# Four moves in the order of work of a two-layer transformer kernel: GpSimd's products, the output projection's sum, the expert mixes, and the third query/key product

## The chip, the cores and the metric

The kernel runs on one core of a Trainium2 chip. The metric is the device time of one execution in microseconds (us). The core's engines are TensorE (PE in the profile; PEld is its weight load), VectorE (DVE), ScalarE (ACT), GpSimd (POOL) and SyncE (SP), which issues the DMAs. They run side by side, each through its own list of instructions in order, and meet at semaphores only.

## The reference

The input is 16 sequences ("rows") of 256 tokens by 128 features. Two layers follow, each an attention and a mixture of experts, with a residual sum and a layer norm behind each of the four parts. All of it is float32.

```python
x = L0_attn_x                                          # (16, 256, 128)
x = _layernorm(x + _L0_attn_ref(...))                  # RMS norm, 16 heads of 64, softmax, output projection, bias
x = _layernorm(x + _L0_ffn_ref(...))                   # a shared expert and 8 routed ones, top 2, hidden 256, gelu
x = _layernorm(x + _L1_attn_ref(...))                  # per token of (b, n, h, d): 16 heads of 8
x = _layernorm(x + _L1_ffn_ref(...))                   # 8 routed experts, top 2, hidden 512, gelu
```

```python
def _layernorm(x, axis=-1, eps=1e-05):
    m = jnp.mean(x, axis=axis, keepdims=True)
    v = jnp.var(x, axis=axis, keepdims=True)
    return (x - m) / jnp.sqrt(v + eps)
```

The second attention mixes the 16 heads of each token with one another (its scores are 16x16 for a token), so it needs no product over tokens and lies on DVE and POOL.

## The kernel before

**Pipeline over rows.** The rows go through a software pipeline of 18 iterations. Iteration `it` does, for three rows at once, part a (first attention and the up products of the first experts) of row `it`, part b (down products of the first experts, second attention, up products of the second experts) of row `it-1`, and part c (down products of the second experts) of row `it-2`. Iterations 2 to 14 are one hardware loop of 13 passes; 0, 1, 15, 16 and 17 are written out, with the parts that exist there (part a ends with iteration 15).

**Steps.** Within an iteration come eight steps `s` (0 to 7), one for each pair of heads of the first attention: scores `S{2s+2}`, `S{2s+3}` of the next pair (PE), their negated maxima `head_max` (DVE), `softmax_exp` (ACT), transposes `T` of the probabilities (PE), their copy (ACT), the product `O{s}` with the values (PE), its copy to `oT` (ACT, `o_out`), its scaling by the inverse sums (DVE, `o_scale`, L662), and the query/key product `QK{s+3}` (PE) with its split in two parts (ACT `qk_out`, DVE `lower_qk`). Between these PE does "fill" units of parts b and c: `D0p0` to `D0p3` and `D1e0` to `D1e7` are the down products of experts, which DVE weighs by the gates and adds up (`mix`, L723). `fill_out(v, s, place)` (L817) says which mixes belong to which place of a step.

**Behind the steps.** `OUT` is the output projection: 16 products of 128x128, of 8 head pairs for each of 2 blocks of tokens, summed in one PSUM bank (L1018 to L1026). DVE adds the residual `x_plus` (input plus bias, made on POOL in `plus`, L445) and takes the layer norm's statistics (`ln_stats`); POOL turns the variance into its inverse root (`inverse_std`, L424); DVE applies both (`ln_apply`, L693, its instruction is L696); PE transposes the result (`X1T`), DVE splits it in two parts (L809, L814), and the up products `U0_0` to `U0_8` follow. In between lie `D1e6`, `D1e7`, the value products `V0` to `V3` of the next row, the second attention's `AOT` and `PROJ`, its norm's transpose `X3T`, then `QK0`, `QK1` and the up products `U1_0` to `U1_15`.

**What sets the order.** PE's order is the list that `pe_units` (L62) writes; the orders of the other engines are written out in their bodies: POOL's at L477, DVE's at L828. Each PSUM bank has two semaphores, `filled` and `drained`: a unit waits until the bank's last user is drained. Banks are given in rings: `A0`, `A1` for `QK`, `O`, `HT`, `OUT`, `V`, `X1T`; `F0`, `F1` for the fill units (with `T0`, `T1` behind the steps). So `D0p3` uses the bank of `D0p2` and waits until the mix of `D0p2` has read it, and `O6` uses the bank of `O5` and waits for `o_scale(5)`.

**POOL's part of the second attention.** `value_product(v, t, halves)` (L468) multiplies the weights of one block `t` of tokens by the values, one instruction of 128x1024 for each half of the heads; those of block 1 are L471 with no sum behind them, and DVE sums them in `head_mix(v, 1, ·)`, behind the mix of `D1e7`.

Of the kernel before, what the change touches and what calls it, by code (L numbers as in the profile page):

```python
# [36 lines left out]
NT = S // P  # L37
# [24 lines left out]
def pe_units(it):  # L62

    a, b, c, nxt = it < ROWS, 1 <= it <= ROWS, 2 <= it <= ROWS + 1, it < ROWS - 1
    order = []
    rings = {"A": ["A0", "A1"], "F": ["F0", "F1"], "G": ["F0", "F1", "T0", "T1"]}
    turn = {"A": 0, "F": 0, "G": 1}

    def put(ring, *names, on=True):
        for name in names if on else ():  # L70
            banks = rings.get(ring, [ring])
            order.append((name, banks[turn.get(ring, 0) % len(banks)]))
            if ring in turn:
                turn[ring] += 1

    put("F", "D0p0", "D0p1", on=b)
    for s in range(HP):
        put("S0", f"S{2 * s + 2}", on=a and s + 1 < HP)
        put("S1", f"S{2 * s + 3}", on=a and s + 1 < HP)
        put("A", "QK2", on=a and s == 0)  # L80
        put("A", f"O{s - 1}", on=a and s >= 1)
        put("F", *fill_units(it, s, 0))
        put("T0", f"T{2 * s}", on=a)
        put("T1", f"T{2 * s + 1}", on=a)
        put("A", f"QK{s + 3}", on=a and s + 3 < HP)
        put("A", "HT", on=nxt and s == HP - 2)
        put("F", *fill_units(it, s, 1))
    put("A", f"O{HP - 1}", "OUT", on=a)
    put("F", "D1e6", "D1e7", on=c)
    put("A", "V0", on=nxt)  # L90
    put("A", "X1T", on=a)
    put("G", "V1", on=nxt)
    put("A", "V2", on=nxt)
    put("G", "U0_0", "U0_1", on=a)
    put("A", "R0", on=a)
    put("G", "U0_2", "U0_3", on=a)
    put("G", "AOT", on=b)
    put("G", "U0_4", on=a)
    put("G", "PROJ", on=b)
    put("G", "U0_5", "U0_6", "U0_7", "U0_8", on=a)  # L100
    put("A", "V3", on=nxt)
    put("G", "X3T", on=b)
    put("A", "QK0", "QK1", on=nxt)
    put("G", "U1_0", "U1_1", "U1_2", "R1", "U1_3", "U1_4", on=b)
    put("G", "U1_5", "U1_6", on=b)
    put("S0", "S0", on=nxt)
    put("S1", "S1", on=nxt)
    put("G", *[f"U1_{u}" for u in range(7, 2 * E)], on=b)
    return order
# [71 lines left out]
def transformer_blocks(nc, x_in, norm_scale, wq_in, wk_in, wv_in, wo_in, b_out_in,  # L181
# [3 lines left out]
    with ctx:  # L185
# [221 lines left out]
        @block.gpsimd  # L407
        def _(pool):
            g = nc.gpsimd
            g.memset(ident[:], 0.0).then_inc(consts_ready, 1)  # L410
            pool.wait_ge(consts_ready, 1)
            g.affine_select(out=ident[:], in_=ident[:], compare_op=ALU.not_equal, fill=1.0, base=0,
                            pattern=[[-1, P]], channel_multiplier=1)
            g.memset(minus_half[:], -0.5)
            g.memset(table_load[:], 0.0)
            for i in range(2):
                g.memset(top2[i][:], -3.0e38)
                g.memset(gates[i][:, :, E:E + 1], 1.0)
            g.memset(ln_eps[:], LN_EPS)
            g.memset(rms_eps[:], RMS_EPS)  # L420
            g.memset(one_over_d[:], 1.0 / D).then_inc(consts_ready, 1)
            pool.wait_ge(consts_ready, 2)

            def inverse_std(v, i, lag):  # L424
                pool.wait_ge(stats_ready[i], v.at(lag, 1, 1))
                settled(pool, g.tensor_tensor(var_eps[i][:], mv[i][:, :, 1], ln_eps[:], ALU.add))  # L426
                g.tensor_tensor(std_inv[i][:], var_eps[i][:], minus_half[:], ALU.pow).then_inc(std_ready[i], 1)  # L427

            def split_up_weights(group, *weights):

                pool.wait_ge(loaded[group], n_loads[group])
                for whole, (w_hi, _) in weights:
                    g.tensor_copy(w_hi[:], whole)
                pool.drain()
                for whole, (w_hi, w_lo) in weights:
                    ins = g.tensor_tensor(w_lo[:], whole, w_hi[:].bitcast(F32), ALU.subtract)  # L436
                ins.then_inc(up_split, 1)

            def rms(v):
                pool.wait_ge(sq_ready, v.at(-1, 1, 1))  # L440
                settled(pool, g.tensor_tensor(mean_sq[:], sum_sq[:], one_over_d[:], ALU.mult))  # L441
                settled(pool, g.tensor_tensor(mean_sq[:], mean_sq[:], rms_eps[:], ALU.add))
                g.tensor_tensor(rms_inv[:], mean_sq[:], minus_half[:], ALU.pow).then_inc(rms_ready, 1)  # L443

            def plus(v):  # L445
                wait_weights(pool, v, 1)
                pool.wait_ge(x_loaded, v.at(-1, 16, 16))
                if v.a:
                    pool.wait_ge(*v.drain("OUT"))
                g.tensor_tensor(x_plus[:], x_row[:], b_out[:, 0:1, :].broadcast_to([P, NT, D]), ALU.add).then_inc(xplus_ready, 1)  # L450

            def head_product(v):


                for t, i in ((0, 1), (1, 0), (1, 1))[0 if v.a else 1:]:
                    if (t, i) != (1, 1):
                        pool.wait_ge(*v.drain(f"LQ{t}"))
                    q, k = head_pairs(t, half(i))
                    settled(pool, g.tensor_tensor(prod[:, t, half(i)], q, k, ALU.mult))  # L459
                    ins = add_pairs(prod[:, t, half(i)], DH1)  # L460
                    if i == 1:
                        ins.then_inc(prod_ready, 1)

            def add_pairs(x, n):

                return g.tensor_tensor(x[:, :, :, 0:n // 2], x[:, :, :, 0:n // 2], x[:, :, :, n // 2:n], ALU.add)  # L466

            def value_product(v, t, halves=(0, 1)):  # L468
                pool.wait_ge(exp1_ready, v.at(1, NT, t + 1))
                for i in halves:  # L470
                    ins = g.tensor_tensor(pv1[:, t, half(i)], *weights_and_values(t, i), ALU.mult)  # L471
                    if t == 0:
                        pool.drain()  # L473
                    ins = add_pairs(pv1[:, t, half(i)], NH1) if t == 0 else ins
                    ins.then_inc(pv1_ready, 1)

            def body(v):  # L477
                if v.it == 0:
                    split_up_weights(2, (router0_in_sb[:], router0), (up0_loaded, up0))
                if v.next:  # L480
                    rms(v)
                if v.it == 0:
                    split_up_weights(4, (up1_loaded, up1))
                if v.b:
                    wait_weights(pool, v, 3)
                    inverse_std(v, 1, 1)
                    pool.wait_ge(ln_ready[1], v.at(1, 1, 1))
                    g.tensor_tensor(x3[:], x2[:], bproj[:, 0:1, :].broadcast_to([P, NT, D]), ALU.add).then_inc(x2plus_ready, 1)  # L488
                    head_product(v)
                    if v.a:  # L490
                        value_product(v, 0)
                    value_product(v, 1, (0,))
                if v.a:
                    inverse_std(v, 0, 0)
                if v.b:
                    value_product(v, 1, (1,))
                if v.c:
                    inverse_std(v, 3, 2)
                if v.b:
                    inverse_std(v, 2, 1)  # L500
                if v.next:
                    plus(v)

            def before(v):
                rms(v)
                plus(v)

            run(pool, body, before)
# [136 lines left out]
        def _(dve):  # L645
# [182 lines left out]
            def body(v):  # L828
# [5 lines left out]
                for s in range(HP):  # L834
# [5 lines left out]

                    if v.a and s + 2 < HP:
                        lower_qk(v, s + 2)
                    if v.a and s >= 1:
                        o_scale(v, s - 1)
                    if v.b and s == 0:
                        mix(v, "D0p1", 0, (2, 3), x2, x1, not v.a)
                    if s not in (0, 3, HP - 1):
                        fill_out(v, s - 1, 1)
                    fill_out(v, s, 0)
                    if v.a and s + 1 < HP:  # L850
                        inverse_sums(v, s + 1)
# [91 lines left out]
        def _(pe):  # L943
# [3 lines left out]
            def tokens(t):  # L947
                return slice(t * P, (t + 1) * P)
# [39 lines left out]
            def unit(v, name):  # L988
# [29 lines left out]
                if name == "X3T":  # L1018
                    wait_weights(pe, v, 4)
                if name == "OUT":  # L1020
                    for t in range(NT):
                        for s in range(HP):
                            if t == 0 and s == HP - 1:
                                wait_drained(v, name, f"O{s}")
                            ins = te.matmul(bank[:, tokens(t)], oT[:, s, tokens(t)], wo[:, s, :], start=s == 0, stop=s == HP - 1)
                    return ins  # L1026
                if name[0] == "O":
                    s = int(name[1:])
# [128 lines left out]
```

## Time and profile before

| | |
|---|---|
| median of 3 runs | 1565.22 us (1562.77 to 1567.48) |
| the profiled execution: its time | 1567.07 us |
| its span | 1565.3 us |
| mean granted TensorE clock | 0.976 |
| busy: PE | 1421.9 us, 91% |
| busy: PE weight load | 1249.4 us, 80% |
| busy: DVE | 985.5 us, 63% |
| busy: ACT | 860.9 us, 55% |
| busy: POOL | 514.5 us, 33% |

The table is from the page's first part. Busy shares are means over stages; an engine that is 91% busy has waits somewhere, and what a change in one place is worth is read from the wait that ends last there. Idle time in square brackets behind a row of the timeline is the time in which that engine stood idle before the row, and what ended it. A matmul's row lasts until its modelled end, which overlaps the next one's start: the spacing of starts is what a matmul costs in a stream. Each float32 product of 128x128 is two rows of the records.

### The profile page before, as it was taken

The page shows a single profiled execution, that of the slowest core. Times are in us where ns is not written, and L with a number is a line of the kernel's source. Part 1 is how long each engine was busy: PE and PEld are TensorE (multiplying, and loading weights), DVE is VectorE, ACT ScalarE, POOL GpSimd, SP SyncE. Part 2 cuts the span into 40 slices and gives each one's busy share as a digit, 9 for nine tenths or more (in the row PEclk, how much of TensorE's full clock was granted, in tenths as well). Part 3 has the DMA queues.
Part 4 walks back from the last instruction along what each step waited for, and adds up shares of the span by engine and source line. Part 5 has one row for each costly group of instructions (what it writes and reads, how often), then busy time and mean ns, then how long its engine had stood idle before and what let it go on. Part 6 is the DMA issues. An engine that isn't in the chain of part 4 may idle for free.

```text
span 1565.3 us, 34497 instructions
## 1 busy us (share of the span) xinstructions
PE 1421.9 (91%) x12096; PEld 1249.4 (80%) x12096; DVE 985.5 (63%) x2534; ACT 860.9 (55%) x2361; POOL 514.5 (33%) x415
## 2 busy tenths in 40 slices
PE   6897999999999999999999999999999999998847
PEld 5675888888888888878888888888888887887747
DVE  4456576675757667575666757667575766757482
ACT  5564655656465564647556464655646465463403
POOL 3206061340605134060522506043250614315040
PEclk9898999999999999999999999999999999998978
DMA  7000000000000000000000000000000000000000
GB/s 239 4 2 1 5 2 8 0 7 0 0 7 0 7 0 7 0 0 7 0 7 0 7 0 0 7 0 7 0 1 5 0 7 0 3 1 1 4 1 7
DMA packets 14088, 13.78 MB, mean 9 GB/s; under 512 B 1625, under 2 KB 12770, under 8 KB 13794
## 3 DMA queue, kind: packets, MB, share of 16 engines
q1 hardware_dynamic: 14050, 13.27, 2.6%
q8 instruction: 24, 0.39, 0.1%
q14 instruction: 14, 0.11, 0.0%
HBM read 11.17 MB, written 2.10 MB: 8 GB/s over the span
## 4 chain that ended last, share of the span: by engine, by line
issue 62%; POOL 17%; POOLq 14%; PE 4%; DVE 1%; ACT 1%; DMA 0%; DVEq 0%; SPq 0%
POOLq L329 8%; POOL hid L466 6%; POOL hid L471 6%; POOLq L473 5%; POOL std_inv L427 2%; PE bank_F L1101 1%; POOL up_lo L436 1%; POOL x L488 1%; POOL x_plus L450 1%; POOL rms_inv L443 1%; PE bank_S L983 0%; DMA b_out<-in_b_out 0%; ACT probs L544 0%; DVE hid L743 0%; DVE hid L761 0%
## 5 line engine op out<-in xcount | busy, mean ns | idle before, releaser
L1101 PE MATMUL bank_F<-down,hid 128*128 128x128 f32 x3072 | 374.9, 278 | 34.6 <-DVE x L731 34.0
L1101 PEld LDWEIGHTS bank_F<-down,hid 128*128 128x128 f32 x3072 | 359.4, 193 | 46.3 <-DVE x L731 38.1
L544 ACT ACTIVATE probs<-bank_S,neg_max 128x256 f32<-128x256 f32 x512 | 235.5, 475 | 179.0 <-DVE neg_max L652 178.9
L652 DVE TENSOR_REDUCE neg_max<-bank_S 128x2 f32<-128x512 f32 x256 | 164.6, 684 | 83.5 <-PE bank_S L983 80.2
L471 POOL TENSOR_TENSOR hid<-hid,qkv 128x1024 f32<-128x1024 f32 x62 | 177.1, 2857 | 47.1 <-ACT hid L560 47.1
L731 DVE SCALAR_TENSOR_TENSOR x<-bank_F,gates,x 128x128 f32<-128x128 f32 x512 | 155.2, 345 | 31.6 <-PE bank_F L1101 21.4
L523 ACT ACTIVATE probsT<-bank_T 128x512 f32<-128x512 f32 x256 | 139.6, 605 | 44.1 <-PE bank_T L1012 44.0
L426 POOL TENSOR_TENSOR var_eps<-mv,ln_eps 128x2 f32<-128x2 f32 x64 | 12.5, 195 | 428.5 <-DVE mv L690 428.5
L441 POOL TENSOR_TENSOR mean_sq<-sum_sq,one_over_d 128x2 f32<-128x2 f32 x16 | 3.1, 194 | 455.1 <-ACT h_row L518 455.1
L1012 PE MATMUL bank_T<-ident,probs 128*128 128x128 f32 x1024 | 138.4, 279 | 0.1
L459 POOL TENSOR_TENSOR hid<-qkv 128x1024 f32<-128x1024 f32 x47 | 112.2, 2386 | 66.6 <-ACT qkv L523 66.6
L1040 PE MATMUL bank_A<-probsT,values 128*64 128x256 f32 x1024 | 133.5, 382 | 0.4 <-ACT probsT L523 0.4
L1012 PEld LDWEIGHTS bank_T<-ident,probs 128*128 128x128 f32 x1024 | 113.8, 142 | 23.4 <-issue 21.3
L572 ACT ACTIVATE hid<-bank_T 128x512 f32<-128x512 f32 x141 | 84.2, 598 | 75.5 <-PE bank_T L971 60.4
L466 POOL TENSOR_TENSOR hid<-hid 128x512 f32<-128x512 f32 x77 | 112.8, 1465 | 10.9
L969 PE MATMUL bank_T<-x1T_hi,up_lo 128*128 128x256 f32 x378 | 114.4, 303 | 0.4
L665 DVE TENSOR_TENSOR oT<-oT,bank_A 128x256 f32<-128x256 f32 x128 | 53.6, 419 | 97.0 <-ACT oT L532 95.9
L971 PE MATMUL bank_T<-x1T_hi,up_hi 128*128 128x256 f32 x378 | 107.8, 285 | 0.0
L970 PE MATMUL bank_T<-x1T_lo,up_hi 128*128 128x256 f32 x378 | 107.8, 285 | 0.0
L544 ACT ACTIVATION_READ_ACCUMULATOR probs<-bank_S,neg_max 128x1 f32 x512 | 105.9, 207 | 0.0
L983 PE MATMUL bank_S<-qk_hi,qk_lo 64*128 64x256 f32 x512 | 86.5, 333 | 17.1 <-ACT probs L544 12.5
L572 ACT ACTIVATE hid<-bank_F 128x512 f32<-128x512 f32 x115 | 68.7, 598 | 50.4 <-PE bank_F L971 33.7
(167 smaller groups left out, 3259.1 us busy)
## 6 DMA issues: line engine op xcount, KB each, us to landing
x_row<-in_x SPq DMA_DIRECT2D x16, 128.0 KB, 2.1
down<-in_w SPq DMA_DIRECT2D x1, 2048.0 KB, 14.0
out<-x SPq DMA_DIRECT2D x16, 128.0 KB, 1.8
hid<-in_w SPq DMA_DIRECT2D x1, 1536.0 KB, 7.8
hid<-in_rw SPq DMA_DIRECT2D x1, 1024.0 KB, 6.6
hid<-in_wv SPq DMA_DIRECT2D x1, 512.0 KB, 3.8
hid<-in_wq SPq DMA_DIRECT2D x1, 512.0 KB, 4.7
hid<-in_wk SPq DMA_DIRECT2D x1, 512.0 KB, 5.6
```

The lines of the kernel that those rows point to most:

```text
L329: eng.drain()
L466: return g.tensor_tensor(x[:, :, :, 0:n // 2], x[:, :, :, 0:n // 2], x[:, :, :, n // 2:n], ALU.add)
L471: ins = g.tensor_tensor(pv1[:, t, half(i)], *weights_and_values(t, i), ALU.mult)
L523: sc.activation(dst, src, ACT.Copy).then_inc(v.drain(name)[0], 1)
L544: ins = sc.activation(probs[:, h // 2 % 2, h % 2, t, :], unit.bank(f"S{h}")[:, t * S:(t + 1) * S], ACT.Exp, bias=neg_max[:, h, t:t + 1], a ...
L572: sc.activation(hid1[:, e, m:m + 2, :], v.bank(f"U1_{u}")[:, :].rearrange("p (m n) -> p m n", m=2), ACT.Gelu).then_inc(v.drain(f"U1_{u}")[ ...
L652: ve.tensor_reduce(neg_max[:, h, :], v.bank(f"S{h}")[:, :].rearrange("p (t k) -> p t k", t=NT), AX.X, ALU.max, negate=True).then_inc(max_r ...
L731: ins = ve.scalar_tensor_tensor(acc[:, t, :], y[:, j, t, :], gates[i][:, t, e:e + 1], src[:, t, :], ALU.mult, ALU.add)
L969: te.matmul(out, s_lo, m_hi, start=True, stop=False)
L1012: ins = te.transpose(bank[:, k * S + t * P:k * S + (t + 1) * P], probs[:, h // 2 % 2, h % 2, t, tokens(k)], ident[:])
L1040: ins = te.matmul(bank[r, 0:S], values[:, k, s * P + j * DH:s * P + j * DH + DH], probsT[:, j, k, :], start=k == 0, stop=k == NT - 1)
L1101: ins = te.matmul(bank[:, (j * NT + t) * P:(j * NT + t + 1) * P], hid[:, e, k, tokens(t)], down[:, e, k, :], start=k == 0, stop=k == m - 1)
```

## The change

It makes five edits, and no instruction is added or taken away but for some register and wait instructions.

1. **POOL, L489 to L502.** Both halves of `value_product(v, 1)` stand ahead of `inverse_std(v, 0, 0)`; before, the second half stood behind it.
2. **POOL, same place.** `plus(v)` stands right behind `inverse_std(v, 0, 0)`, with a wait of its own for `ln_ready[0]` (which `ln_apply(v, 0, ...)` on DVE sets); before, it was the last of the iteration.
3. **DVE, L840 to L848.** `o_scale(v, s - 1)` stands behind the mixes of `D0p1` and of `fill_out(v, s - 1, 1)`; before, ahead of them. That changes something in steps 1 (`D0p2`), 2 (`D0p3`), 5 (`D1e1`) and 6 (`D1e2`).
4. **PE, L76 to L80.** `QK2` stands ahead of `S2` and `S3`.
5. **PE, L1020 to L1025.** `OUT` goes over head pairs outside and token blocks inside, so the wait for `O7` stands ahead of the last 2 of 16 products; before, ahead of the eighth. One start flag clears the bank for both blocks.

```diff
+        put("A", "QK2", on=a and s == 0)
         put("S0", f"S{2 * s + 2}", on=a and s + 1 < HP)
         put("S1", f"S{2 * s + 3}", on=a and s + 1 < HP)
-        put("A", "QK2", on=a and s == 0)
         put("A", f"O{s - 1}", on=a and s >= 1)
...
-                    value_product(v, 1, (0,))
+                    value_product(v, 1)
                 if v.a:
                     inverse_std(v, 0, 0)
-                if v.b:
-                    value_product(v, 1, (1,))
+                if v.next:
+                    pool.wait_ge(ln_ready[0], v.at(0, 1, 1))
+                    plus(v)
                 if v.c:
                     inverse_std(v, 3, 2)
                 if v.b:
                     inverse_std(v, 2, 1)
-                if v.next:
-                    plus(v)
...
-                    if v.a and s >= 1:
-                        o_scale(v, s - 1)
                     if v.b and s == 0:
                         mix(v, "D0p1", 0, (2, 3), x2, x1, not v.a)
                     if s not in (0, 3, HP - 1):
                         fill_out(v, s - 1, 1)
+                    if v.a and s >= 1:
+                        o_scale(v, s - 1)
                     fill_out(v, s, 0)
...
-                    for t in range(NT):
-                        for s in range(HP):
-                            if t == 0 and s == HP - 1:
-                                wait_drained(v, name, f"O{s}")
-                            ins = te.matmul(bank[:, tokens(t)], oT[:, s, tokens(t)], wo[:, s, :], start=s == 0, stop=s == HP - 1)
+                    for s in range(HP):
+                        if s == HP - 1:
+                            wait_drained(v, name, f"O{s}")
+                        for t in range(NT):
+                            ins = te.matmul(bank[:, tokens(t)], oT[:, s, tokens(t)], wo[:, s, :], start=s == t == 0, stop=(s, t) == (HP - 1, NT - 1))
```

POOL in the loop, from the first product of token block 1 to the norm statistics of part c; `hid<-hid,qkv` is a value product. Before:

```order
L471 TENSOR_TENSOR hid<-hid,qkv 128x1024 [waits exp1_ready]
L425 REGISTER_ALU
L426 TENSOR_TENSOR var_eps<-mv,ln_eps 128x2 [waits stats_ready0]
L427 TENSOR_TENSOR std_inv<-var_eps,minus_half 128x2
L471 TENSOR_TENSOR hid<-hid,qkv 128x1024 [waits exp1_ready]
L425 REGISTER_ALU
L426 TENSOR_TENSOR var_eps<-mv,ln_eps 128x2 [waits stats_ready3]
```

And now:

```order
L471 TENSOR_TENSOR hid<-hid,qkv 128x1024 [waits exp1_ready]
L471 TENSOR_TENSOR hid<-hid,qkv 128x1024
L425 REGISTER_ALU
L426 TENSOR_TENSOR var_eps<-mv,ln_eps 128x2 [waits stats_ready0]
L427 TENSOR_TENSOR std_inv<-var_eps,minus_half 128x2
L447 REGISTER_ALU [waits ln_ready0]
L449 ISA [waits x_loaded]
L450 TENSOR_TENSOR x_plus<-x_row,b_out 128x256 [waits drained_A1]
L425 REGISTER_ALU
L426 TENSOR_TENSOR var_eps<-mv,ln_eps 128x2 [waits stats_ready3]
```

The second product went from behind the inverse root to ahead of it, and the sum `x_plus` came up from the end of the iteration, behind a wait for the applied norm.

DVE in step 1 of the loop: `qk_lo` is `lower_qk`, `oT` is `o_scale(0)`, the four `x<-bank_F,gates,x` are the mix of `D0p2`. Before:

```order
L652 TENSOR_REDUCE neg_max<-bank_S 128x2 [waits filled_S1]
L670 REGISTER_ALU
L671 TENSOR_TENSOR qk_lo<-bank_A,qk_hi 128x512 [waits qk_rounded]
L665 TENSOR_TENSOR oT<-oT,bank_A 128x256 [waits o_copied]
L731 SCALAR_TENSOR_TENSOR x<-bank_F,gates,x 128x128 [waits filled_F0]
L731 SCALAR_TENSOR_TENSOR x<-bank_F,gates,x 128x128 x3
L660 RECIPROCAL row_inv<-row_sum 128x4 [waits drained_S1,drained_S0]
```

And now:

```order
L651 TENSOR_REDUCE neg_max<-bank_S 128x2 [waits filled_S1]
L669 REGISTER_ALU
L670 TENSOR_TENSOR qk_lo<-bank_A,qk_hi 128x512 [waits qk_rounded]
L730 SCALAR_TENSOR_TENSOR x<-bank_F,gates,x 128x128 [waits filled_F0]
L730 SCALAR_TENSOR_TENSOR x<-bank_F,gates,x 128x128 x3
L664 TENSOR_TENSOR oT<-oT,bank_A 128x256 [waits o_copied]
L659 RECIPROCAL row_inv<-row_sum 128x4 [waits drained_S1,drained_S0]
```

The mix and the scaling changed places; `row_inv` stays behind both.

PE at `OUT`, from its first product to the first fill unit behind it. Before:

```order
L1025 MATMUL bank_A<-wo,oT 128x128 [waits drained_A1]
L1025 MATMUL bank_A<-wo,oT 128x128 x6
L960 REGISTER_ALU
L1025 MATMUL bank_A<-wo,oT 128x128 [waits drained_A0]
L1025 MATMUL bank_A<-wo,oT 128x128 x8
```

And now:

```order
L1024 MATMUL bank_A<-wo,oT 128x128 [waits drained_A1]
L1024 MATMUL bank_A<-wo,oT 128x128 x13
L959 REGISTER_ALU
L1024 MATMUL bank_A<-wo,oT 128x128 [waits drained_A0]
L1024 MATMUL bank_A<-wo,oT 128x128
```

The wait for the last scaling (`drained_A0`) moved from behind 7 products to behind 14.

## Rows read from the trace of the kernel before

**Rows 1.** Stretches; one pass of the loop: us, busy (xinstructions) of PE, PEld, DVE, ACT, POOL, PEclk, DMA

```profile
328.00:420.21 92.21, 87.12 (x760) 76.81 (x758) 60.33 (x158) 53.19 (x147) 31.65 (x25) 1.00 0.01 3
```

**Rows 2.** Timeline, PE behind the steps: start us, us, engine, line, what xcount [idle <-releaser]

```profile
415.37 1.83 PE L1025 MATMUL bank_A<-wo,oT 128*128 128x128 f32 x14
418.10 2.27 PE L1025 MATMUL bank_A<-wo,oT 128*128 128x128 f32 x18 [0.90 <-DVE oT L665]
420.21 3.74 PE L1101 MATMUL bank_F<-down,hid 128*128 128x128 f32 x32
...
424.25 0.39 PE L971 MATMUL bank_A<-wv_hi,hT_hi 128*128 128x512 f32 x1
426.20 0.44 PE L953 MATMUL bank_A<-ident,x 128*128 128x128 f32 x2 [1.56 <-DVE x L696]
...
427.92 0.39 PE L969 MATMUL bank_T<-x1T_hi,up_lo 128*128 128x256 f32 x1
...
436.33 0.40 PE L971 MATMUL bank_A<-wv_hi,hT_hi 128*128 128x512 f32 x1
437.04 0.41 PE L953 MATMUL bank_F<-ident,x 128*128 128x128 f32 x2 [0.31 <-DVE x L696]
```

**Rows 3.** Timeline, PE in steps 0 and 1, and at O6 of the pass before

```profile
407.83 0.66 PE L1033 MATMUL bank_A<-ident,row_inv 128*64 128x128 f32 x8 [0.28 <-DVE oT L665]
...
456.83 0.39 PE L983 MATMUL bank_S<-qk_hi,qk_lo 64*128 64x256 f32 x2 [0.65 <-ACT probs L544]
...
457.73 0.39 PE L969 MATMUL bank_A<-hT_hi,wq_lo 128*128 128x256 f32 x1
...
458.55 1.03 PE L1012 MATMUL bank_T<-ident,probs 128*128 128x128 f32 x8
...
466.04 0.28 PE L971 MATMUL bank_A<-hT_hi,wk_hi 128*128 128x256 f32 x1
467.64 2.05 PE L1101 MATMUL bank_F<-down,hid 128*128 128x128 f32 x16 [1.32 <-DVE x L731]
```

**Rows 4.** Timeline, DVE: around OUT and the two norms, then in step 1

```profile
402.06 0.42 DVE L665 TENSOR_TENSOR oT<-oT,bank_A 128x256 f32<-128x256 f32 x1 [1.08 <-ACT oT L532]
...
417.62 0.42 DVE L665 TENSOR_TENSOR oT<-oT,bank_A 128x256 f32<-128x256 f32 x1
420.41 0.42 DVE L800 TENSOR_TENSOR x<-bank_A,x_plus 128x256 f32<-128x256 f32 x1 [2.37 <-PE bank_A L1025]
...
423.46 2.68 DVE L696 TENSOR_SCALAR x<-x,mv,std_inv 128x128 f32<-128x128 f32 x2
...
435.89 1.00 DVE L696 TENSOR_SCALAR x<-x,mv,std_inv 128x128 f32<-128x128 f32 x2 [0.38 <-POOL std_inv L427]
...
465.96 0.42 DVE L665 TENSOR_TENSOR oT<-oT,bank_A 128x256 f32<-128x256 f32 x1 [1.08 <-ACT oT L532]
466.30 1.29 DVE L731 SCALAR_TENSOR_TENSOR x<-bank_F,gates,x 128x128 f32<-128x128 f32 x4
```

**Rows 5.** Source L696, ln_apply's instruction in all norms: ns min/median/max

```profile
L696 DVE TENSOR_SCALAR x<-x,mv,std_inv x128: 313/340/2772, 70.3 to 1562.7; 128x128 f32<-128x128 f32 x128
```

**Rows 6.** Timeline, POOL around the first norm and at the end of the pass

```profile
415.40 2.79 POOL L471 TENSOR_TENSOR hid<-hid,qkv 128x1024 f32<-128x1024 f32 x1
421.98 0.20 POOL L426 TENSOR_TENSOR var_eps<-mv,ln_eps 128x2 f32<-128x2 f32 x1 [3.79 <-DVE mv L690]
422.99 2.81 POOL L471 TENSOR_TENSOR hid<-hid,qkv 128x1024 f32<-128x1024 f32 x1
...
435.82 0.73 POOL L450 TENSOR_TENSOR x_plus<-x_row,b_out 128x256 f32<-128x256 f32 x1
```

**Rows 7.** Timeline, PE at X1T in iterations 1 and 15, which stand outside the loop

```profile
147.75 0.66 PE L953 MATMUL bank_A<-ident,x 128*128 128x128 f32 x2 [5.25 <-DVE x L696]
...
1439.71 0.66 PE L953 MATMUL bank_A<-ident,x 128*128 128x128 f32 x2 [2.37 <-DVE x L696]
```

**Rows 8.** Stretch behind X1T of iteration 15, columns as in rows 1

```profile
1440.00:1450.00 10.00, 8.89 (x43) 8.56 (x42) 5.48 (x13) 3.35 (x8) 0.00 (x0) 0.51 0.00 0
```

## The prediction

> **What bounds the kernel now.** I read the stretches of one pass of the loop first, then PE's timeline for its idle gaps, then the timeline of the engine that ends each gap. A pass takes 92.2 us, PE is busy for 87.1 of them at a granted clock of 1.00, DVE for 60.3, ACT 53.2, POOL 31.7 [rows 1]. So PE bounds the loop, and what can be won without taking work from it are its 5.0 us of idle time. They are six waits: 0.90 within `OUT`, 1.56 before `X1T`, 0.31 before `X3T` [rows 2], 0.28 before `O6`, 0.65 before `S2`, 1.32 before `D0p3` [rows 3]. Their sum is 5.02, all of it. The change touches five of the six. It takes no work from any engine, so its worth is how much of these gaps it closes, less the waits that take their place. The listed idle time is a little too small as a price: a matmul's row ends at its modelled end, which in a stream overlaps the next. I therefore price a gap by starts: when the unit starts, against when it would in a stream.
>
> **OUT by steps (edit 5).** Of 32 rows 14 start before the wait and 18 behind it; 18 take 420.21 - 418.10 = 2.11 us, 0.117 each [rows 2]. In a stream 32 take 3.75, so `D1e6` would start at 415.37 + 3.75 = 419.12 in place of 420.21. The last scaling ends at 417.62 + 0.42 = 418.04 [rows 4]; 28 rows are through at 415.37 + 28 x 0.117 = 418.65. No wait is left: **-1.09**. The residual on DVE, which waits for `OUT`, comes as much earlier, at 419.3, and so do the norm's statistics, which POOL takes up at 421.98 now [rows 6] and at 420.9 then.
>
> **The product ahead of the statistics (edit 1).** `ln_apply`'s two instructions take 2.68 us here [rows 4], where the median of one is 0.34 [rows 5], about 0.6 for the pair. They end at 426.14, just behind the POOL product of 422.99 to 425.80 [rows 6]: it holds them up. Ahead of the inverse root it would start at 418.19, end at 421.0, and meet statistics ready at 420.9. I expect it a little earlier: in step 5 DVE idles 1.08 us before `o_scale` [rows 4], the mix of `D1e1` (two instructions, half of the four that take 1.29) now fits in, and the chain from there over the head exponentials to POOL moves up by some 0.5. Product end 420.5, then, with 0.4 to spare. The inverse root is ready 1.0 later, as now (421.98 to 422.99), at 421.9; DVE gets to `ln_apply` 1.09 earlier, at 422.4, and ends at 423.0. PE reaches `X1T` one start (0.23) behind the last of `V0`, 424.25 + 0.23 - 1.09 = 423.39. So `X1T` starts at 423.39, where it starts at 426.20: 2.81 earlier, of which 1.09 are counted. **-1.72**. Everything up to `U0_0` hangs on `X1T` as before (1.72 later, 427.92), on PE and on DVE, so I carry the whole gain along.
>
> What runs beside the product in its new place is the scaling, the residual and the statistics. The scaling of 417.62 lies within today's first product (415.40 to 418.19) and takes 0.42, as the one at 402.06 [rows 4]: not held up. For the statistics no row shows it. The bounds are 0 and a residual held until the product's end at 421.0 in place of 419.3, 1.7. I take 0, since its nearest row, the scaling, has one operand in the banks and one in SBUF like the residual. The Trainium skill (SBUF, Who interferes with whom) has a rule: a DVE instruction contends with GpSimd's if it has two inputs in SBUF or runs in a mode that uses two ports, as a `tensor_scalar` can, and whichever starts first blocks the other. By it the norm's application is blocked, as the rows show (2.68 against 0.6), and residual and statistics (one SBUF input each) are not, so the term would be 0; were it wrong, 1.7.
>
> **x_plus in the middle (edit 2).** `x_plus` runs at 435.82 and beside it `ln_apply` of part b takes 1.00 [rows 4, 6] in place of 0.6. Moved away, it lets `X3T` start 0.4 earlier than 437.04; PE could have it at 436.33 + 0.23 = 436.56. **-0.40**. In its new place it waits for the applied norm, so it cannot block that. Behind it POOL waits for statistics ready some 10 us later; nobody is held. SP's queue issues the next row's load once `x_plus` is done, some 12 us sooner, with no store near: 0.
>
> **QK2 first (edit 4).** `S2` waits for the exponentials of the last pair until 456.83, 0.65 after PE is free at 456.18. `QK2` takes 458.55 - 457.73 = 0.82 [rows 3]. Put in the gap it ends at 457.00, `S2` starts 0.17 later than now, the next unit at 457.90 in place of 458.55: **-0.65**. `S2`'s followers on DVE lose 0.17; the copy of `QK2` on ACT gains over 1.
>
> **Mixes ahead of scaling (edit 3).** `D0p3` starts at 467.64, in a stream it would at 466.04 + 0.12 = 466.16. It waits for the mix of `D0p2` (466.30, 1.29 us), which stands behind a scaling that itself waited 1.08 for ACT until 465.96 [rows 3, 4]. The mix can start at 464.88 then and end at 466.17: `D0p3` at 466.23, **-1.41**. That is nearly a tie. The price is paid by `o_scale`: in steps 1 and 2 its bank is needed some microseconds later, cost 0. In step 6 `O6` already waits for it, and the mix of `D1e2` (0.6) now stands ahead; but DVE comes to step 6 some 0.5 earlier, since `D1e1` filled a wait. Bounds: 0 and +0.6. I take 0.1.
>
> **Sum.** 1.09 + 1.72 + 0.40 + 0.65 + 1.41 = 5.27 a pass, less 0.1 for `O6` and 0.1 for the ties: 5.07; 13 passes give 65.9. Iteration 1 has the same stall of `D0p3`, and at `X1T` 5.25 us [rows 7], of which the held-up norm is about 2.0: with the smaller ones 4.3. Iteration 15 waits 2.37 at `X1T` [rows 7], and behind it the granted clock is 0.51, the lower level of 1.2 GHz, for some 10 us [rows 8]. There the gaps are worth 1.4 + 3.0, and if the clock stays up half of that stretch's PE time less the waits behind it, about 3.5: 7.9. Iteration 0 gives 0.4, as its `ln_apply` is beside `x_plus` too. Iterations 16 and 17 have no first attention and no edit in play. Together 78.5. The profiled execution took 1567.07, so it would take 1488.6; against the median, 1565.22, **1486.7 us**.
>
> **Rivals.**
> *A, the scaling pays (0.2).* DVE does not get to step 6 earlier, `O6` starts 0.6 later, and the tie at `D0p3` goes the wrong way by 0.5, as its mix starts only when `lower_qk` is through. Against it: the 1.08 of idle time before the scaling in both steps [rows 4]. 14 x 1.1 = 15 less gain: 1502.
> *B, the product is in the way (0.1).* It ends behind the statistics, or holds up the residual: 1.7, less 0.4 to spare at `X1T`, 15 x 1.3 = 20 less: 1507. For it: 421.0 against 420.9 without the shift.
> *C, no change (0.05).* The edits do not bring what they say, since the loop's pace is set by a ring through DVE and ACT and each closed gap opens behind the next unit. Against it: DVE's 60 busy us of 92. Time 1562 to 1568.
> *D, slower (0.05).* One mechanism at `X1T`: the second product, started late, ends 2 us or more behind the statistics, so `X1T`'s gap is not 1.72 but 3.2, and the clock falls in every pass as it does behind 2.37 us of waiting in iteration 15 [rows 7, 8]; behind 1.56 it stays at 1.00 [rows 1, 2]. Then a pass keeps 5.27 - 1.72 = 3.55, and loses 1.5 and the 3.5 of a slow stretch: +1.5 x 13 and nothing gained at the edges, about 1584. It decides at a product end of 423 where I have 420.5. The Trainium skill (TensorE: Matmul & The Clock Gate, Part 1) has the lower clock as the default state and activity as what releases it; by that rule closed gaps can only help the clock, and the trace agrees, with 1.00 and 0.51 behind the short and the long wait.
>
> **Numbers.** The forecast itself has 0.6, and by its own terms lies between 1478 (all ties won, 5.5 a pass, 13 at the edges) and 1496 (4.7 a pass, 7 at the edges). The range reaches over A and to the edge of B, 1477 to 1508. A measurement of this kernel can tell 0.3% (4.7 us) from no change. Faster: forecast, A and B, 0.9; same: C, 0.05; slower: D, 0.05.
>
> **What would show it.** In the profile after: a pass of 87.1 us with PE busy for about 86.5; the first norm's `ln_apply` pair at 0.6 in place of 2.68 with the product ended before it; part b's at 0.6 in place of 1.00; no idle time listed within `OUT`, before `X1T`, `S2` and `D0p3`, and 0.3 to 0.4 left before `O6`. Wrong would be a pass above 88.5, a new wait of PE above 0.5, a `var_eps` of the first norm that waits for POOL and not for DVE, or a clock below 1.00 in the loop.

## The result and the profile after

| | before | after |
|---|---|---|
| median | 1564.06 us (4 runs) | 1472.02 us (4 runs, 1470.65 to 1474.68) |
| ratio, 95% interval | | 0.941 (0.9389 to 0.9432) |
| span of the profiled execution | 1565.3 us | 1470.9 us |
| mean granted TensorE clock | 0.976 | 0.986 |
| busy: PE, DVE, ACT, POOL | 1421.9, 985.5, 860.9, 514.5 us | 1395.0, 942.5, 865.2, 515.5 us |

The kernel is 6% faster, and its time lies below the low end of the range (1477). By the medians the gain is 92.0 us; the two profiled executions, 1567.07 and 1472.66 us, are 94.4 apart. A pass of the loop, from the stretches of the kernel after (columns as in [rows 1]), with a stretch of iteration 1 (from POOL's `mean_sq` in it to that of iteration 2) and one of iteration 15 (behind `X1T`):

```profile
100.19:183.97 83.78, 73.98 (x630) 63.52 (x632) 51.31 (x136) 53.36 (x147) 30.69 (x24) 0.98 0.01 3
...
615.64:701.94 86.30, 86.01 (x758) 76.67 (x760) 57.50 (x158) 53.50 (x147) 31.70 (x26) 1.00 0.01 3
...
1351.00:1385.00 34.00, 28.39 (x221) 26.66 (x222) 17.16 (x67) 18.56 (x38) 1.78 (x4) 1.00 0.02 5
```

The pass went from 92.2 to 86.3 us and PE's idle time in it from 5.1 (92.21 - 87.12; the six listed waits, which the prediction took for all of it, sum to 5.02) to 0.3 us. The whole program has the same number of matmul rows, 12096, before and after. Of the six waits one is left, the one before `O6` (645.88). The timeline of PE in the kernel after, at the places of [rows 2, 3]:

```profile
645.88 0.66 PE L1032 MATMUL bank_A<-ident,row_inv 128*64 128x128 f32 x8 [0.29 <-DVE oT L664]
...
653.42 3.84 PE L1024 MATMUL bank_A<-wo,oT 128*128 128x128 f32 x32
657.09 3.74 PE L1100 MATMUL bank_F<-down,hid 128*128 128x128 f32 x32
...
661.14 0.39 PE L970 MATMUL bank_A<-wv_hi,hT_hi 128*128 128x512 f32 x1
661.37 0.38 PE L952 MATMUL bank_A<-ident,x 128*128 128x128 f32 x2
...
663.02 0.28 PE L968 MATMUL bank_T<-x1T_hi,up_lo 128*128 128x256 f32 x1
663.13 0.28 PE L969 MATMUL bank_T<-x1T_lo,up_hi 128*128 128x256 f32 x1
...
671.25 0.39 PE L970 MATMUL bank_A<-wv_hi,hT_hi 128*128 128x512 f32 x1
671.54 0.41 PE L952 MATMUL bank_F<-ident,x 128*128 128x128 f32 x2
...
686.88 3.73 PE L1100 MATMUL bank_F<-down,hid 128*128 128x128 f32 x32
690.37 0.36 PE L968 MATMUL bank_A<-hT_hi,wq_lo 128*128 128x256 f32 x1
...
693.01 0.36 PE L968 MATMUL bank_A<-hT_hi,wq_lo 128*128 128x256 f32 x1
...
699.71 0.27 PE L970 MATMUL bank_A<-hT_hi,wk_hi 128*128 128x256 f32 x1
699.83 2.05 PE L1100 MATMUL bank_F<-down,hid 128*128 128x128 f32 x16
```

`OUT` is one row of 32 with no wait in it. `X1T` (661.37) starts 0.23 behind the last product of `V0`, `X3T` (671.54) 0.29 behind that of `V3`, `QK2` (690.37) stands where `S2`'s wait was, and `D0p3` (699.83) starts 0.12 behind the last product of `QK4`.

The timeline of DVE in the kernel after, at the places of [rows 4]:

```profile
657.29 0.43 DVE L799 TENSOR_TENSOR x<-bank_A,x_plus 128x256 f32<-128x256 f32 x1 [1.72 <-PE bank_A L1024]
657.81 0.66 DVE L687 BATCH_NORM_STATS2 stats<-x 128x6 f32<-128x128 f32 x2
...
660.35 0.60 DVE L695 TENSOR_SCALAR x<-x,mv,std_inv 128x128 f32<-128x128 f32 x2
...
670.79 0.60 DVE L695 TENSOR_SCALAR x<-x,mv,std_inv 128x128 f32<-128x128 f32 x2 [0.39 <-POOL std_inv L427]
...
698.48 1.28 DVE L730 SCALAR_TENSOR_TENSOR x<-bank_F,gates,x 128x128 f32<-128x128 f32 x4
```

And POOL, at the places of [rows 6]:

```profile
652.94 5.60 POOL L471 TENSOR_TENSOR hid<-hid,qkv 128x1024 f32<-128x1024 f32 x2
658.87 0.20 POOL L426 TENSOR_TENSOR var_eps<-mv,ln_eps 128x2 f32<-128x2 f32 x1 [0.34 <-DVE mv L689]
...
661.19 0.74 POOL L450 TENSOR_TENSOR x_plus<-x_row,b_out 128x256 f32<-128x256 f32 x1 [1.28 <-DVE x L695]
```

The two products end at 658.54, and the inverse root then waits 0.34 for DVE, so POOL is in time. The mix of `D0p2` ends at 699.76, 0.07 ahead of `D0p3`, the near tie that was forecast. `ln_apply`'s pair takes 0.60 in both norms. The row of its source line answers to [rows 5]; its longest was 2772 ns and is now 349:

```profile
L695 DVE TENSOR_SCALAR x<-x,mv,std_inv x128: 314/342/349, 69.8 to 1468.3; 128x128 f32<-128x128 f32 x128
```

### The profile page after: what moved, and what is told of

The parts are those of the page before. It is cut to its first block, busy times and chain, and to the rows that moved or that the text cites. A ratio compares the mean times of both kernels' runs of the same rounds, so it can differ in the third digit from the quotient of the medians.

```text
span 1470.9 us, 34497 instructions
## 1 busy us (share of the span) xinstructions
PE 1395.0 (95%) x12096; PEld 1237.2 (84%) x12096; DVE 942.5 (64%) x2534; ACT 865.2 (59%) x2361; POOL 515.5 (35%) x415
## 4 chain that ended last, share of the span: by engine, by line
PE 68%; issue 12%; DVE 10%; POOL 4%; ACT 3%; POOLq 2%; DVEq 1%; DMA 0%; SPq 0%; ACTq 0%
PE bank_F L1100 16%; PE bank_S L982 5%; PE bank_T L1011 4%; PE bank_A L1039 4%; PE bank_A L1024 3%; PE bank_T L968 3%; DVE hid L742 3%; PE bank_T L969 3%; PE bank_T L970 3%; PE bank_A L1032 3%; PE bank_A L969 3%; PE bank_A L968 3%; PE bank_A L970 3%; PE bank_F L968 2%; DVE neg_max L651 2%
## 5 line engine op out<-in xcount | busy, mean ns | idle before, releaser
L441 POOL TENSOR_TENSOR mean_sq<-sum_sq,one_over_d 128x2 f32<-128x2 f32 x16 | 3.2, 197 | 448.6 <-ACT h_row L517 448.6
```

## The experiments

A pass is measured in all of them as the mean distance of POOL's `mean_sq` instruction (L441, once for each row of the input) over 11 passes: 92.15 us before, 86.32 after. "After" in this section is the changed kernel, and each diff is against it.

**Each edit undone by itself.** This asks what a closed gap was worth with the other four edits in place. Each version ran twice. The diffs are cut to what moves, in the order of the edits; in the third `o_scale` goes ahead of the mix of `D0p1` as well, and in the fifth the wait for `O7` goes ahead of the eighth product.

```diff
-value_product(v, 1)
+value_product(v, 1, (0,))
 inverse_std(v, 0, 0)
+value_product(v, 1, (1,))
```

```diff
-    pool.wait_ge(ln_ready[0], v.at(0, 1, 1))
-    plus(v)
...
 inverse_std(v, 2, 1)
+plus(v)
```

```diff
+o_scale(v, s - 1)
 fill_out(v, s - 1, 1)
-o_scale(v, s - 1)
```

```diff
-put("A", "QK2", on=a and s == 0)
 put("S0", f"S{2 * s + 2}", on=a and s + 1 < HP)
 put("S1", f"S{2 * s + 3}", on=a and s + 1 < HP)
+put("A", "QK2", on=a and s == 0)
```

```diff
-for s in range(HP):
-    for t in range(NT):
+for t in range(NT):
+    for s in range(HP):
```

> The change without edit 1 (second product behind the inverse root again). Theory G (each edit closes its own gap of PE, priced by starts, and the prices add): the norm's application is held up by the product again, X1T starts 1.7 us later, a pass of the loop is 86.3 + 1.7 = 88.0 us. Theory J (the edits need each other, the whole is more than its parts): edits 2 to 5 alone close less, a pass above 88.6.

> The change without edit 2 (x_plus at the end of POOL's iteration). Theory G: the second norm's application takes 1.0 us again in place of 0.6, X3T starts 0.4 us later, a pass is 86.7 us. Theory J: the load of the next row, 12 us later, or the queue matters too, a pass above 87.0. Theory N (nobody waits for it): 86.3.

> The change without edit 3 (scaling ahead of the mixes in all steps). Theory G: D0p3 waits again, 1.5 us, and the product on POOL ends 0.5 us later, which costs nothing to 0.1: a pass of 87.8 to 87.9 us. Theory J: the product's later end makes X1T wait as well, 88.2 or more. O6 waits 0.3 as before in both.

> The change without edit 4 (QK2 behind S2 and S3). Theory G: S2 waits 0.65 listed again, by starts 0.8: a pass of 87.1 us. Theory J: with QK2 late the copy on ACT and the exponentials behind it come 1 us later, and D0p3 waits too, a pass above 87.5.

> The change without edit 5 (OUT by token blocks outside). Theory G: PE waits 0.9 listed within OUT again, by starts 1.2: a pass of 87.5 us, and POOL's product ends well ahead of the statistics. Theory J: above 88.

| undone | time us | ratio to before, 95% | pass us | longer by | term of the forecast |
|---|---|---|---|---|---|
| 1, product | 1509.07 | 0.9643 (0.9615 to 0.9671) | 88.31 | 1.99 | 1.72 |
| 2, x_plus | 1478.40 | 0.9447 (0.9420 to 0.9474) | 86.71 | 0.39 | 0.40 |
| 3, mixes | 1496.71 | 0.9564 (0.9529 to 0.9599) | 87.79 | 1.47 | 1.41 |
| 4, QK2 | 1484.64 | 0.9487 (0.9453 to 0.9521) | 87.08 | 0.76 | 0.65 |
| 5, OUT | 1481.43 | 0.9465 (0.9447 to 0.9484) | 86.97 | 0.65 | 1.09 |

With edit 1 undone, the timeline shows the old picture, the product beside `ln_apply` and `X1T` behind it (line numbers are 2 higher than in the kernel after):

```profile
584.09 2.82 POOL L471 TENSOR_TENSOR hid<-hid,qkv 128x1024 f32<-128x1024 f32 x1
584.56 2.69 DVE L697 TENSOR_SCALAR x<-x,mv,std_inv 128x128 f32<-128x128 f32 x2
...
587.31 0.44 PE L954 MATMUL bank_A<-ident,x 128*128 128x128 f32 x2 [1.56 <-DVE x L697]
```

With edit 2 undone, part b's `ln_apply` runs beside `x_plus` and takes 1.01, and `X3T` waits 0.32:

```profile
586.36 0.74 POOL L450 TENSOR_TENSOR x_plus<-x_row,b_out 128x256 f32<-128x256 f32 x1
586.44 1.01 DVE L694 TENSOR_SCALAR x<-x,mv,std_inv 128x128 f32<-128x128 f32 x2 [0.39 <-POOL std_inv L427]
...
587.59 0.41 PE L951 MATMUL bank_F<-ident,x 128*128 128x128 f32 x2 [0.32 <-DVE x L694]
```

With edit 3 undone `D0p3` waits 1.33 again, and with edit 4 undone `S2` waits 0.65. So each edit closes the gap it was made for. Edit 5 alone is off: worth 0.65 where its gap is more than 1. With it undone, `OUT`'s wait is 0.38 and not 0.90, since the last scaling (570.59) ends 2.16 us behind `OUT`'s start, where in [rows 2, 4] it is 417.62 + 0.42 - 415.37 = 2.67:

```profile
568.85 1.83 PE L1024 MATMUL bank_A<-wo,oT 128*128 128x128 f32 x14
570.59 0.42 DVE L664 TENSOR_TENSOR oT<-oT,bank_A 128x256 f32<-128x256 f32 x1
...
571.06 1.16 PE L1024 MATMUL bank_A<-wo,oT 128*128 128x128 f32 x8 [0.38 <-DVE oT L664]
```

The five sum to 5.26, and the whole change gained 5.83. Two theories stood for the missing 0.57: edits 3 and 5 cover for each other (H), or edit 5 is simply worth 0.65 and the rest of `OUT`'s gap went with the product (I).

**Edits 3 and 5 undone together** (both edits of the list above in one kernel).

> Edits 3 and 5 undone together, on the change. Alone, edit 3 undone cost 1.47 us a pass and edit 5 undone 0.65, where the gaps they closed measure 1.48 and 1.17. Theory H (they help each other: with the mix ahead, DVE reaches the last scaling about 0.5 us earlier, so the half of OUT's gap is closed by edit 3 alone): undone together they cost the whole 1.48 + 1.17 = 2.65, the pass is 86.32 + 2.65 = 88.97, OUT's wait is 0.9 again as in [rows 2], the time 1472.0 + 13 x 2.65 + some at the edges = about 1508. Theory I (edit 5 is simply worth 0.65, the other 0.5 of OUT's gap went with the product, edit 1): the costs add to 2.12, pass 88.44, OUT's wait 0.4, time about 1500. Above both (over 89.3): the two touch a third wait.

Measured 1512.90 us (ratio to before 0.9658, 0.9643 to 0.9673), a pass of 88.99: 2.67 longer, where H said 2.65 and I said 2.12. `OUT`'s wait is back at 0.90, and the last scaling ends 2.67 behind `OUT`'s start:

```profile
581.34 1.83 PE L1026 MATMUL bank_A<-wo,oT 128*128 128x128 f32 x14
583.59 0.42 DVE L664 TENSOR_TENSOR oT<-oT,bank_A 128x256 f32<-128x256 f32 x1
...
584.07 1.16 PE L1026 MATMUL bank_A<-wo,oT 128*128 128x128 f32 x8 [0.90 <-DVE oT L664]
```

H holds. Half of `OUT`'s gap is closed twice over, by a scaling that comes 0.5 earlier (edit 3) and by a wait that stands later (edit 5). With that 0.55 the sum is 5.81 of 5.83.

**The product made late on purpose.** To test the mechanism of rival D, POOL does the second half's product once, or twice, more ahead of the statistics. The extra products write what is there already. Each of the two versions ran once. The lines stand in `value_product` behind the product, with n = 1 and then 2.

```diff
+if v.a and (t, i) == (1, 1):
+    for _ in range(n):
+        pool.drain()
+        ins = g.tensor_tensor(pv1[:, t, half(i)], *weights_and_values(t, i), ALU.mult)
```

> The change with POOL's second product of block 1 written twice (2.8 us more on POOL ahead of the norm's inverse root, same values). Theory L (only the wait grows): the root comes 2.5 us later, X1T waits 2.2 us, a pass is 88.5 us at a clock of 1.00. Theory D (rival D of the prediction: behind such a wait the clock falls): the clock in the 10 us behind X1T is near 0.5 and a pass is 91 to 92 us.

> The same product written three times (5.6 us more on POOL). Theory L: X1T waits 5 us, a pass is 91.3 us at a clock of 1.00. Theory D: the clock falls as in iteration 1 of the kernel before (behind 5.25 us), a pass is 94 us or more.

One more product: 1511.36 us, a pass of 88.44, `X1T` waits 1.69 and the granted clock of the pass stays at 1.00. The product ends at 586.99 and the statistics, ready at 584.3, wait for it (timeline, line numbers 4 higher):

```profile
584.05 0.25 DVE L693 BATCH_NORM_AGGREGATE mv<-stats 128x2 f32<-128x6 f32 x2
584.16 2.83 POOL L475 TENSOR_TENSOR hid<-hid,qkv 128x1024 f32<-128x1024 f32 x1
...
588.73 0.44 PE L956 MATMUL bank_A<-ident,x 128*128 128x128 f32 x2 [1.69 <-DVE x L699]
```

Two more: 1576.42 us, above the 1564.16 to 1566.84 of the kernel before in the same comparison. `X1T` waits 4.56:

```profile
613.04 0.69 PE L956 MATMUL bank_A<-ident,x 128*128 128x128 f32 x2 [4.56 <-DVE x L699]
```

And in the stretches of that kernel (a pass, then 4 us behind `X1T`) the clock behind `X1T` is 0.50, the lower level of 1.2 GHz:

```profile
562.58:655.48 92.90, 88.04 (x750) 78.31 (x751) 59.28 (x157) 52.77 (x143) 37.21 (x27) 0.96 0.01 3
613.04:617.00 3.96, 3.96 (x13) 3.37 (x14) 3.36 (x8) 1.20 (x2) 0.73 (x1) 0.50 0.00 0
```

From one to two the wait grew by 2.87 and the pass shown by 4.46 (88.44 to 92.90); the rest, 1.6, is PE's busy time, which rose from 86.47 to 88.04 at the lower clock. The mean of 11 passes is 93.02, 4.58 more; single passes take 92.3 to 93.9, though `X1T` waits 4.54 to 4.59 in all of them. Neither theory had the size: the wait alone (L) was to give 91.3, the fall of the clock (D) 94 or more. So rival D's mechanism exists in this kernel, at 1.6 to 1.7 us a pass in the mean behind 4.56 us of waiting. The change leaves 0.34 us of POOL's time before its first stage, a longer wait at `X1T`.

**The price of mixing first.** The wait before `O6` is the last one left. Here the scaling stands ahead of the mix in step 6 alone, and then in steps 5 and 6 (`s in (5, 6)` in both conditions).

```diff
+if v.a and s >= 1 and s == 6:
+    o_scale(v, s - 1)
...
-if v.a and s >= 1:
+if v.a and s >= 1 and not (s == 6):
     o_scale(v, s - 1)
```

> The change with the scaling ahead of the mix in step 6 alone (DVE still comes to step 6 earlier, as the mix of D1e1 fills step 5's wait). The price at O6 that the prediction set at 0 to 0.6: if the wait for O6 (0.29 listed) is due to the order in step 6, the scaling comes 0.5 us earlier, the wait is gone and a pass is 85.9 to 86.0 us. If it is due to the exponentials or PE itself, a pass stays at 86.3.

> The change with the scaling ahead of the mixes in steps 5 and 6, where the pass of 85.95 us had it so in step 6 alone. What D1e1's place in step 5 brings: Theory J (the shift matters): o_scale(4) goes back to 1.08 us of waiting and the mix behind it, DVE reaches step 7 about 0.5 later, the second product ends 0.5 later as well, OUT's wait of some 0.3 comes back, X1T stays without a wait of more than 0.3; the pass is 86.2 to 86.5, the time 1469 to 1474. Theory K (the shift has slack everywhere): no new wait, the pass 85.9 to 86.0, the time within 2 us of the version with step 6 alone, 1466. If the product became late, X1T would wait 0.5 or more and the pass exceed 86.6.

> The change with the scaling ahead of the mix in step 6 alone, measured once more beside the change itself on one chip. The first measurement gave a pass of 85.95 us against 86.32, and 1465.8 us against 1472.0. If the 0.37 a pass is O6's wait (0.29, its start 0.37 later than in a stream), the trace shows again no idle time before O6, and the time is 13 to 14 x 0.37 = 4.8 to 5.2 below the change's: 1466 to 1467.5. If the difference was one between chips, it is within 2 us of the change's.

> The change itself once more, the partner of the version with the scaling first in step 6. Both theories: pass 86.3, time 1471 to 1474, O6's wait 0.29. If it comes out at 1467 or less, the gain put down to step 6 was one of the chip.

| | time us | ratio to before, 95% | pass us | wait before `O6` |
|---|---|---|---|---|
| step 6 | 1465.84 | 0.9365 (0.9349 to 0.9381) | 85.95 | none |
| step 6, again | 1466.59 | 0.9363 (0.9351 to 0.9376) | 85.95 | none |
| after, again | 1472.98 | 0.9399 (0.9386 to 0.9412) | 86.32 | 0.29 |
| steps 5 and 6 | 1472.66 | 0.9403 (0.9388 to 0.9417) | 86.29 | 0.27 |

The timeline of the version with step 6, in which `O6`'s bank comes free at 558.12 and PE is there at 558.33:

```profile
557.71 0.41 DVE L664 TENSOR_TENSOR oT<-oT,bank_A 128x256 f32<-128x256 f32 x1
...
558.33 0.66 PE L1034 MATMUL bank_A<-ident,row_inv 128*64 128x128 f32 x8
```

And that of steps 5 and 6, where DVE waits 1.07 in step 5 and comes late to step 6:

```profile
551.09 0.42 DVE L664 TENSOR_TENSOR oT<-oT,bank_A 128x256 f32<-128x256 f32 x1 [1.07 <-ACT oT L531]
...
556.40 0.41 DVE L664 TENSOR_TENSOR oT<-oT,bank_A 128x256 f32<-128x256 f32 x1
...
556.86 0.66 PE L1034 MATMUL bank_A<-ident,row_inv 128*64 128x128 f32 x8 [0.27 <-DVE oT L664]
```

So filling step 5's wait wins the wait before `O6`, and the mix ahead of the scaling in step 6 gives it back. Theory J had the size of steps 5 and 6 right (86.2 to 86.5) but not the place: `OUT`'s wait stayed away, since edit 5 covers it, and `O6` waited instead. Step 6 alone is the fastest version: in one comparison on one chip its five runs lie at 1465.44 to 1468.24 and the change's at 1470.00 to 1474.65, 6.4 us or 0.4% apart by the medians. The 0.37 a pass makes 4.9 of it. The fourth combination, mix first in step 6 without the filled wait in step 5, was not run.

## Why the prediction was wrong, point by point

The direction came out, the five gaps closed by the mechanism that was forecast, and none of the signs named as wrong showed. The size did not: 78.5 us were forecast, the medians differ by 92.0 and the profiled spans by 94.4. The steps that failed are terms of the sum that were sized too small, in the pass (5.07 forecast, 5.83 measured) and at the edges (12.6 forecast, 17.6 and 18.6 in two profiled executions of the change).

**The pass: 5.07 forecast, 5.83 measured**, 9.9 us over 13 passes. By starts:

| term | forecast | measured | from |
|---|---|---|---|
| `OUT` | 1.09 | 1.17 | 4.84 [rows 2], 657.09 - 653.42 = 3.67 |
| `X1T` | 1.72 | 1.72 | 1.95 [rows 2], 661.37 - 661.14 = 0.23 |
| `X3T` | 0.40 | 0.42 | 0.71 [rows 2], 671.54 - 671.25 = 0.29 |
| `QK2`, `S2` | 0.65 | 0.77 | `D0p0` to `QK3`: 459.34 - 452.44 = 6.90, 693.01 - 686.88 = 6.13 |
| `D0p3` | 1.41 | 1.48 | 1.60 [rows 3], 699.83 - 699.71 = 0.12 |
| `O6` | +0.1 | 0 | 0.28 [rows 3], 0.29 after |
| ties | +0.1 | 0 | no wait at `OUT`, `X1T`, `D0p3` |
| not in the forecast | 0 | about 0.3 | units behind `X1T`, 0.18 of it at `U0_0` |

Three things make up the 0.76. (1) "I therefore price a gap by starts" was right, but the time in a stream was taken too long: 3.75 for `OUT`, where it takes 3.67, and the term for `QK2` counted from the modelled end of `D0p0` and `D0p1` at 456.18, so it came out as the listed 0.65 and not as 0.77. With `D0p3` and `X3T` these are about 0.3. (2) The margin of 0.2 for `O6` and the ties was not needed. DVE did get to step 6 earlier, which the forecast argued and then took only in part. (3) "Everything up to `U0_0` hangs on `X1T` as before", so "I carry the whole gain along" took the stretch behind `X1T` as unchanged. It got shorter by about 0.3, with no idle time listed for PE. Of this, 0.18 lies at `U0_0` and goes with a wait of the weight load, which the forecast did not look at. `U0_0`'s first load waits for `x1T_lo` before, and does not wait after:

```profile
427.92 0.19 PEld L969 LDWEIGHTS bank_T<-x1T_hi,up_lo 128*128 128x128 f32 x1 [0.32 <-DVE x1T_lo L814]
```

`X1T` then came straight behind `ln_apply`, while DVE still had a sum and a reciprocal (L771, L772) to do before it split `X1T`'s result. In the kernel after, `X1T` starts later behind the norm, and the split begins 0.41 behind `X1T` in place of 0.74. So `U0_0` starts 1.65 behind `X1T` and not 1.72, and its second product 0.11 behind its first and not 0.22. This is so, to 0.02, in all 12 passes that were read of each kernel, and with edit 1 undone the old values are back; its 1.99 is 1.72 and these pieces. The other 0.1 is spread over units further on and stays open. The rows of before that are not in [rows 2, 3], from PE's timeline:

```profile
428.14 0.28 PE L970 MATMUL bank_T<-x1T_lo,up_hi 128*128 128x256 f32 x1
...
452.44 3.73 PE L1101 MATMUL bank_F<-down,hid 128*128 128x128 f32 x32
...
459.34 0.36 PE L969 MATMUL bank_A<-hT_hi,wq_lo 128*128 128x256 f32 x1
```

**X1T (edit 1): right to 0.01**, and POOL stood idle for 0.34 before the statistics, where 0.4 to spare was argued. The disputed bound was 0 for the residual and the statistics beside POOL's product. They take 0.43 and 0.66 and lie inside it (657.29 to 658.47, the product to 658.54). Before, no product ran beside them (one ended at 418.19, the next began at 422.99 [rows 6]), and they took 0.42 [rows 4] and 0.66 (below). `ln_apply` beside a product takes 2.68 [rows 4]. That agrees with the Trainium skill (SBUF, Who interferes with whom): one input in SBUF is not blocked, a `tensor_scalar` in a two-port mode is. No row shows the mode itself. Nothing in the rows would be explained by the other bound.

```profile
420.92 0.66 DVE L688 BATCH_NORM_STATS2 stats<-x 128x6 f32<-128x128 f32 x2
```

**O6 (edit 3): the price was there and was paid by another part of the same edit.** Rival A's first half is false (DVE is earlier), its mechanism is what the version with step 6 alone removes.

**The edges: 12.6 forecast, 18.6 measured, and 17.6 in a second execution of the change.** Between POOL's `mean_sq` markers the kernels differ by 1.35 up to iteration 1's (0.4 forecast), by 6.49 from there to iteration 2's (4.3), and by 16.61 from iteration 14's to the end, of which a pass is 5.83, so 10.8 (7.9). With the profile of the change taken again, the three are 2.05, 6.61 and 8.9. The stretch of iteration 1 before, and in that second execution, and its `X1T` in iteration 15:

```profile
101.54:191.81 90.27, 76.80 (x630) 65.33 (x630) 54.09 (x134) 53.25 (x147) 30.59 (x23) 0.94 0.01 3
```

```profile
99.49:183.15 83.66, 75.19 (x630) 64.38 (x632) 51.35 (x136) 53.25 (x147) 30.67 (x23) 0.96 0.01 3
...
1350.32 0.41 PE L952 MATMUL bank_A<-ident,x 128*128 128x128 f32 x2 [0.33 <-DVE x L695]
```

In iteration 1 PE is busy for 76.80 us before and 73.98 after, at a mean clock of 0.94 and 0.98, for which the forecast had no term. But the second execution has 75.19 at 0.96 in a stretch that is as long (83.66 and 83.78). So the 2.8 us of busy time are not all a gain of the clock, and how the 6.5 divides between clock and waits is open. One wait is known: `X1T`'s, 5.25 [rows 7] before and 3.56 after, 1.7 where 2.0 was forecast.

In iteration 15 the wait at `X1T` fell from 2.37 [rows 7] to 0.34:

```profile
1351.19 0.41 PE L952 MATMUL bank_A<-ident,x 128*128 128x128 f32 x2 [0.34 <-DVE x L695]
```

and behind it the clock is 1.00 over 34 us (0.95 over 37 us in the second execution), where it was 0.51 over the first 10 [rows 8]. From `X1T` to the first product of `PROJ` it takes 6.2 us in both executions of the change, in place of 10.0: 3.8, where the forecast took 3.5. From `X1T` to the end of the kernel it takes 119.7 us, in place of 125.6, but 121.7 (1472.0 - 1350.32) in the second execution. Over the ten profiled executions of kernels that keep edit 1 and add no product, it is 119.7 to 121.9; with edit 1 undone it is 125.4. So the 5.9 of the first pair of profiles is at the upper end of 3.7 to 5.9; the term of 3.5 was right for its stretch and left out what follows. Ahead of `X1T` it is 4.9 against 4.4.

**The rivals.** C and D did not happen. For D the runs give what the forecast had guessed: the clock stays behind 1.69 us in the loop and falls behind 4.56, and costs about 1.6 us there, not 3.5. The Trainium skill (TensorE: Matmul & The Clock Gate, Part 1) has activity as what releases the upper clock, and the runs agree: 1.00 where the gap was closed, 0.50 where it was made long. Where between 1.69 and 4.56 it turns inside the loop was not tried. The length of a wait alone does not settle it: in iteration 0 `X1T` waits 2.80 in both profiled executions of the change, and over the 4 us behind it the granted clock is 0.57 in the first and 1.00 in the second:

```profile
70.54:74.54 4.00, 4.00 (x15) 3.46 (x16) 0.85 (x2) 1.20 (x2) 0.67 (x1) 0.57 0.11 33
```

```profile
71.43:75.43 4.00, 4.00 (x29) 3.73 (x30) 1.02 (x3) 2.66 (x6) 0.65 (x1) 1.00 0.11 33
```

**The range** left out the measured value. Its low end was taken from 5.5 a pass and 13 at the edges as the most that could be won; these make 84.5, and 1565.22 less 84.5 is 1480.7, not the 1478 that it states. The pass gained 5.83 and the edges 17.6 to 18.6, so both were above their bounds. No bound stood for a wait that only the weight load has, or for what follows the first 10 us of the drain.

## What to carry to other kernels

Where an engine is bound and its gaps are closed, price each gap by starts and take the time in a stream from a unit that runs without a wait; here the sum came out at 5.83 where 5.02 of idle time were listed. Read the waits of the weight load as well, and profile a kernel twice before saying what its first and last iterations gained. Edits that touch the same chain are not priced one by one: undo them in pairs before saying what each is worth. An instruction that fills another engine's wait pays in every step behind it, so after such a move look again at each place where the old order was given up. Here one of the four was worth taking back.

## What the runs showed of the hardware that was not expected

- A wait of the weight load can hide behind a TensorE row with no idle time: at `U0_0` it was 0.32 us, and the products there started 0.07 and 0.18 later than without it.
- With POOL's multiplication beside it, a residual sum (0.43) and the norm's statistics (0.66 for two) take what they take alone, while `ln_apply` takes 2.69 (edit 1 undone) in place of 0.60; with the two-operand sum `x_plus` beside it, 1.01. Beside the extra product, DVE's multiplication `ao<-ao,inv`, both operands in SBUF, took 2.19 (at 584.94, one more product) where it takes 0.29 at 659.44 after.
- A late product costs its wait at first, and more than its wait once the clock falls: 2.1 us of the pass for one extra product of 2.8 us, 6.7 for two.
- The same wait of 2.80 us in the same kernel was followed by a granted clock of 0.57 in one execution and of 1.00 in another.
